# Re-ordering the work on four engines where a first graph network hands over to a second

## The chip, the cores and the metric

The kernel runs on one core of one Trainium2 chip. It is a single launch; the metric is the device time in microseconds (us), and the time given is the median of 3 runs. The engines of the core run their own instruction streams and wait for each other through semaphores: PE (TensorE, matrix products and their weight loads), DVE (VectorE), ACT (ScalarE), POOL (GpSimd) and SP (SyncE, which here only issues DMA transfers).

## The reference

The input is 128 graphs of 64 nodes with 384 features, x, and a 0/1 adjacency matrix per graph. Two networks of two layers each run one after the other, and behind each stands a residual sum with a layer norm:

```python
x = _layernorm(x + _L0_gnn_ref(x, adj, ...), axis=-1)
x = _layernorm(x + _L1_gnn_ref(x, adj, ...), axis=-1)
```

A layer of the first network ("gated") computes two bilinear score matrices of the node features, takes one on and above the diagonal and the other below, multiplies exp(scores) by the adjacency and normalises each row; the result averages a linear map of the features; then a layer norm with its own gain and shift, and relu. A layer of the second network ("softmax") takes scores h h^T / sqrt(384), a softmax masked by the adjacency and normalised again, and adds three products: neighbours above the diagonal with one linear map, below it with a second, and the node itself with a third. Again layer norm, gain, shift, relu. All is float32.

## The kernel before

The 8192 rows (nodes) are cut into 8 passes of 2 streams of 512 rows; a stream is 4 tiles (t) of 128 rows, two graphs in each. A unit is one layer on one stream, so a pass has 4 units: layer 0 of stream 0 and of stream 1, then layer 1 of both. All 8 passes of the first network run, then all 8 of the second. The first network's result goes to the memory tensor x1 and from there into the second.

To keep float32 accuracy, each operand of a product is split into a high half (ACT copies it with rounding) and a low half (the rest, by a subtraction on DVE or POOL), and PE sums three products. So each operand goes through the chain PE, DVE, ACT, POOL before PE may use it, and the program is written so that PE computes the value products of one unit while the others prepare the next. The order on each engine is written out by hand; it changes only where the code is changed. The engines meet at semaphores, and an instruction that waits holds everything behind it on its engine.

Names that matter. In the first network `next_turn(k)` on PE transposes block k (of 3) of the second network's first input (x_in to turn); `next_turn_out(k)` on ACT makes its high half in ht, `next_turn_lo(k)` on DVE its low half. `next_scores` waits for all three.

In the second network a unit has 12 value jobs of 9 matmuls on PE (`values(j)`, L1143): tile t = j div 3, side j mod 3 (upper, lower, own). They go through a ring of 4 work banks. `biased_value(j)` (L1437, DVE) reads a bank, adds the bias and frees it for job j + 4. For the first two sides `values_hi(t)` (L1238, ACT) and `values_lo(t)` (L1329, POOL) make the halves. On PE, jobs 0 to 8 are followed by `turn_block` 0 and 1 of the next unit, job 9, `turn_block` 2, jobs 10 and 11, the next unit's scores, and 4 `contexts` tiles (L1155). `turn_block` 2 (L1104) uses the bank of block 0, and waits for `turn_lo(0)` on DVE (L1416), which waits for `turn_out(0)` on ACT (L1201 in layer 0, L1204 in layer 1). The contexts wait for `values_lo` of their tile. `fold_parts` (L1120, L1123) is PE's first work in a unit. `masks` (L1323, POOL) prepares the adjacency masks for a stream, `diagonal` (L1340) the node's own weight.

Three things of the first network are left over when the second begins. The last stream's context (`gated.variances`, `deviations`, `gain_and_shift`), its residual sum (`add_residual`, L793) and the statistics of the sum (`final_stats`, L798) run on DVE between the first biased values of the second. `residual_and_stats(tiles)` issues for some tiles all the sums, then all the statistics. `final_var` (L802 to L807) collects them, POOL takes the root (`gated_final_roots(1)`, L633), DVE makes the offset (`final_offset`, L811), ACT normalises the rows (`gated_normalise(1)`, L507) and SP stores them.

The second network's layer 1 weights (3 matrices, 0: left, 1: right, 2: own) are loaded and split at this place too. `weight_hi(n)` (L1193, ACT, one instruction) and `weight_lo(n)` (L1313, POOL, three). Weight 2 is loaded into the buffer of weight 0, so SP waits for `weight_lo(0)`:

```python
            sp.wait_ge(folded, 1)
            load_weight(0)
            load_weight(1)
            store_last(0)
            sp.wait_ge(split, 1)
            load_weight(2)
            store_last(1)
            sp.wait_ge(split, SIDES)
```

They are used from unit 2 of the first pass on. Before, `weight_hi(0)`, `(1)` and `(2)` and their low halves all stand in unit 1 of the first pass, beside the first unit's end.

## Time and profile before

| | |
|---|---|
| median of 3 runs | 1760.14 us (1759.49 to 1760.24) |
| the profiled execution | 1760.6 us |
| its span, first to last instruction | 1758.8 us |
| PE matmul busy | 1695.9 us, 96% |
| DVE, ACT, POOL busy | 1255.1, 882.7, 825.3 us (71%, 50%, 47%) |
| mean granted TensorE clock | 0.99 of 2.4 GHz |
| second network's first matmuls | 845.90 us |

The profile is one execution. Its page gives each engine's busy share over the span; the two networks follow each other, so the share is a mean over both, and the place where they meet, from some 840 to 920 us, is about 5% of it. There PE's busy time is 17.65, 13.83, 20.00 and 12.87 us in the four 20 us stretches from 840 to 920. The granted clock is what the chip gave TensorE, as a share of 2.4 GHz: 1.00 or 0.50, and a value between the two where a window holds some of each. In a timeline "[2.35 <-DVE b_ht L711]" means that the engine was idle for 2.35 us before this instruction, ended by the named one.

### The profile page before, as it was taken

Reading aid. Unit: us, or ns where it says so; the run is one execution under the profiler, and the core shown is the slowest. Engines: PE = TensorE matmul, PEld = TensorE weight load, DVE = VectorE, ACT = ScalarE, POOL = GpSimd, SP = SyncE. Lnnn points to the kernel's source line nnn. Section 1 sums busy time; section 2 is a strip of 40 time slices with the busy share of each in tenths; the row PEclk is TensorE's granted clock in tenths of the full one; section 3 lists DMA queues with packets and bytes.
Section 4 is the critical chain, followed back from the end, with each engine's and each line's share of the span. In section 5 each row is a group of like instructions: output and inputs, shape, how many; then the busy total and the mean of one; then the engine's idle time right before and its main releaser. Section 6 shows DMA issues by size and latency. Waiting matters only on the chain.

```text
span 1758.8 us, 30529 instructions
## 1 busy us (share of the span) xinstructions
PE 1695.9 (96%) x9856; PEld 1601.9 (91%) x9856; DVE 1255.1 (71%) x2735; ACT 882.7 (50%) x1785; POOL 825.3 (47%) x860
## 2 busy tenths in 40 slices
PE   7999999999999999999889999999999999999994
PEld 6989989898998988998789999999999999999994
DVE  4587685958768586786846867768677686776766
ACT  4545455464545546455445464454554545544542
POOL 5143242424324243334546646666465664656635
PEclk9999999999999999999899999999999999999997
DMA  7014030020202102030111020201202011020200
GB/s 224 1 31 153 6 104 15 24 89 28 91 6 64 55 24 89 6 114 17 49 50 58 21 92 21 92 0 34 80 21 92 0 54 59 21 92 0 75 1 36
DMA packets 76358, 91.98 MB, mean 52 GB/s; under 512 B 29600, under 2 KB 67488, under 8 KB 76320
## 3 DMA queue, kind: packets, MB, share of 16 engines
q1 hardware_dynamic: 76320, 91.51, 15.7%
q8 instruction: 20, 0.33, 0.1%
q14 instruction: 18, 0.15, 0.0%
HBM read 53.75 MB, written 25.17 MB: 45 GB/s over the span
## 4 chain that ended last, share of the span: by engine, by line
PE 38%; issue 36%; POOL 16%; DVE 4%; ACT 3%; SPq 1%; DMA 1%; POOLq 0%; DVEq 0%; ACTq 0%
PE b_work L1143 24%; PE b_work L1155 5%; POOL g_qv_lo L620 3%; POOL b_ht L600 3%; POOL s_v_lo L1329 3%; PE b_work L355 2%; PE b_turn L1104 2%; PE b_score_ps L105 2%; POOL b_z L1353 1%; PE b_work L379 1%; PE b_score_ps L369 1%; POOL g_keep_l L615 1%; POOL b_z L1355 1%; POOL g_sigma L629 1%; POOL g_a_nat L616 1%
## 5 line engine op out<-in xcount | busy, mean ns | idle before, releaser
L1143 PE MATMUL b_work<-b_w_hi,b_ht 128*128 128x384 f32 x2304 | 615.7, 340 | 0.0
L1143 PEld LDWEIGHTS b_work<-b_w_hi,b_ht 128*128 128x128 f32 x2304 | 420.9, 189 | 0.0
L1143 PE MATMUL b_work<-b_w_lo,b_ht 128*128 128x384 f32 x1152 | 387.4, 336 | 0.0
L355 PE MATMUL b_work<-b_ht,b_w_hi 128*128 128x512 f32 x1152 | 357.7, 392 | 9.8 <-DVE b_w_lo L695 9.8
L1329 POOL TENSOR_TENSOR s_v_lo<-s_v_full,s_v_hi 128x384 fp32r<-128x384 f32 x256 | 247.4, 983 | 198.2 <-ACT s_v_hi L1238 197.4
L620 POOL TENSOR_TENSOR g_qv_lo<-g_v_full,g_qv_hi 128x384 fp32r<-128x384 f32 x128 | 133.2, 1060 | 360.5 <-ACT g_qv_hi L493 360.5
L355 PEld LDWEIGHTS b_work<-b_ht,b_w_hi 128*128 128x128 f32 x1152 | 216.2, 189 | 51.2 <-issue 9.7
L355 PE MATMUL b_work<-b_ht,b_w_lo 128*128 128x512 f32 x576 | 225.9, 392 | 0.0
L1143 PEld LDWEIGHTS b_work<-b_w_lo,b_ht 128*128 128x128 f32 x1152 | 218.1, 189 | 0.0
L718 DVE TENSOR_TENSOR g_qv_lo<-b_work,g_qv_hi 128x512 fp32r<-128x512 f32 x192 | 128.7, 687 | 111.9 <-ACT g_qv_hi L481 110.0
L379 PE MATMUL b_work<-b_w_hi,b_ht 128*128 128x384 f32 x768 | 206.5, 336 | 0.0
L1437 DVE TENSOR_TENSOR s_v_full<-b_work,b_bias 128x384 f32<-128x384 f32 x256 | 140.3, 553 | 81.6 <-PE b_work L1143 81.6
L481 ACT ACTIVATE g_qv_hi<-b_work 128x512 fp32r<-128x512 f32 x192 | 110.6, 591 | 132.2 <-PE b_work L355 132.1
L1238 ACT ACTIVATE s_v_hi<-s_v_full 128x384 fp32r<-128x384 f32 x256 | 129.4, 529 | 86.1 <-DVE s_v_full L1437 86.1
L369 PE MATMUL b_score_ps<-g_qv_hi,b_ht 128*128 128x256 f32 x768 | 146.9, 285 | 4.8 <-DVE g_qv_lo L718 4.8
L379 PEld LDWEIGHTS b_work<-b_w_hi,b_ht 128*128 128x128 f32 x768 | 139.9, 188 | 1.3
L355 PEld LDWEIGHTS b_work<-b_ht,b_w_lo 128*128 128x128 f32 x576 | 108.7, 189 | 23.0
L379 PE MATMUL b_work<-b_w_lo,b_ht 128*128 128x384 f32 x384 | 128.8, 335 | 0.0
L369 PEld LDWEIGHTS b_score_ps<-g_qv_hi,b_ht 128*128 128x128 f32 x768 | 120.6, 188 | 8.5 <-DVE g_qv_lo L718 7.4
L1437 DVE TENSOR_TENSOR s_v_own<-b_work,b_bias 128x384 f32<-128x384 f32 x128 | 71.1, 555 | 65.3 <-PE b_work L1143 64.9
L369 PE MATMUL b_score_ps<-g_qv_lo,b_ht 128*128 128x256 f32 x384 | 107.3, 279 | 0.0
L1244 ACT ACTIVATE b_z<-b_z,s_foffset,s_frstd 128x384 f32<-128x384 f32 x62 | 39.0, 699 | 134.8 <-DVE s_foffset L1533 134.8
(138 smaller groups left out, 3225.0 us busy)
## 6 DMA issues: line engine op xcount, KB each, us to landing
b_x_in<-in_x_t SPq DMA_DIRECT2D x16, 768.0 KB, 7.0
g_x_res<-in_x SPq DMA_DIRECT2D x16, 768.0 KB, 7.7
x<-b_z SPq DMA_DIRECT2D x16, 768.0 KB, 3.9
b_x_in<-x SPq DMA_DIRECT2D x16, 768.0 KB, 5.1
s_x_res<-b_x_in SPq DMA_DIRECT2D x16, 768.0 KB, 5.4
out<-b_z SPq DMA_DIRECT2D x15, 768.0 KB, 3.6
b_a_tr<-in_adj_t SPq DMA_DIRECT2D x64, 64.0 KB, 3.4
g_a_nat<-in_adj SPq DMA_DIRECT2D x32, 64.0 KB, 2.5
```

The costliest lines, as they stand in the source:

```text
L355: mm = pe.matmul(bank[:], w, h, start=(n == 0), stop=(n == len(pairs) - 1))
L369: mm = pe.matmul(score_ps[:, t, :, :], h, q, start=(n == 0), stop=(n == len(pairs) - 1))
L379: mm = pe.matmul(bank[:, 0:H], h, w, start=(n == 0), stop=(n == len(pairs) - 1))
L481: nc.scalar.activation(q_hi[:, m, :, d, :], work[use % RING][:], ACT.Copy).then_inc(q_hi_ready, 1)
L600: nc.gpsimd.tensor_tensor(ht_lo[s][:, k, :], xt_in[s][:, k, :], ht_hi[s][:, k, :].bitcast(F32), ALU.subtract).then_inc(x_split, 1)
L620: nc.gpsimd.tensor_tensor(v_lo[:, t, 0:H], v_full[:, t, :], v_hi[:, t, 0:H].bitcast(F32), ALU.subtract).then_inc(v_lo_ready, 1)
L718: op = nc.vector.tensor_tensor(q_lo[:, m, :, d, :], bank, q_hi[:, m, :, d, :].bitcast(F32), ALU.subtract)
L1143: mm = pe.matmul(bank[:, 0:H], h, w, start=(n == 0), stop=(n == len(pairs) - 1))
L1155: mm = pe.matmul(bank[:, 0:HC], p, v, start=(n == 0), stop=(n == len(pairs) - 1))
L1238: nc.scalar.activation(v_hi[:, t, n, 0:H], v_full[:, (2 * t + n) % VF, :], ACT.Copy)\
L1329: nc.gpsimd.tensor_tensor(v_lo[:, t, n, 0:H], v_full[:, (2 * t + n) % VF, :], v_hi[:, t, n, 0:H].bitcast(F32), ALU.subtract).then_inc(v_lo ...
L1437: nc.vector.tensor_tensor(dst, work[(unit * WN + j) % RING][:, 0:H], bias[:, side, layer, :], ALU.add).then_inc(work_free, 1)
```

## The change

It computes the same values with the same instructions. What moves:

- PE: `next_turn(2)` is issued behind the value job of tile 2, ahead of tile 3's, in place of behind it. ACT's `next_turn_out(2)` goes ahead of the last `value_hi`, and DVE's `next_turn_lo(2)` ahead of `probabilities_lo` and the last biased value.
- DVE: the last residual sums and statistics, issued for tiles (0, 1) behind biased value 5 and (2, 3) behind value 7, are now issued tile by tile: tile 0 behind value 6, tile 1 behind the turned block's third low half, tile 2 behind the row sum `own_probability`, tile 3 with `final_var` in the next unit, behind its first biased value. `final_offset` goes behind that unit's `deviations`. DVE's first pass is written out ahead of its loop for this.
- ACT: `weight_hi(0)` goes to unit 0, behind the high halves of tile 1; `weight_hi(1)` to the end of unit 0, in the place of `gated_normalise(1)`; `gated_normalise(1)` into unit 1 behind `probabilities_hi`, where the two weights had been; `weight_hi(2)` behind the turned blocks' copies and the last high halves.
- POOL: `weight_lo(0)` behind `diagonal` of unit 0, the two low halves of tile 2 and then the masks of stream 1 behind it; `weight_lo(1)` at the end of unit 0, in the place of `gated_final_roots(1)`, which goes behind the first low halves of unit 1.
- SP: the same.

```diff
--- before.py
+++ after.py
@@ -416,10 +416,11 @@
                     for t in range(1, NT):
 
                         value(i, unit, t, uses=1 if more or t < NT - 1 else 2)
+                        if not more and t == 2:
+                            next_turn(2)
                     if more:
                         query(i, unit + 1, 0).then_inc(work_full, 1)
                     else:
-                        next_turn(2)
                         next_scores()
                     contexts(i, unit)
                     if more:
@@ -527,12 +528,12 @@
                 value_hi(i, unit, 1)
                 probabilities_hi(i, unit)
                 value_hi(i, unit, 2)
+                if not more:
+                    next_turn_out(2)
                 value_hi(i, unit, 3)
                 if more:
                     query_hi(i, unit + 1, 0)
                     contexts_out(i, unit)
-                else:
-                    next_turn_out(2)
 
             def one_pass(i, last):
 
@@ -849,10 +850,9 @@
                 biased_value(i, unit, 2)
                 if not more:
                     next_turn_lo(1)
+                    next_turn_lo(2)
                 probabilities_lo(i, unit)
                 biased_value(i, unit, 3, uses=1 if more else 2)
-                if not more:
-                    next_turn_lo(2)
                 if s is not None:
                     for t in range(NT - 1):
                         final_stats(i, s, t)
@@ -1256,19 +1256,18 @@
                 exponentials(i, unit)
                 values_hi(i, unit, 0)
 
-            def second_half(i, unit, more, split_weights):
+            def second_half(i, unit, more, tail):
                 values_hi(i, unit, 1)
                 probabilities_hi(i, unit)
-                if split_weights:
-                    weight_hi(0)
-                    weight_hi(1)
+                if tail:
+                    gated_normalise(1)
                 values_hi(i, unit, 2)
-                if split_weights:
-                    weight_hi(2)
                 if more:
                     for k in range(KO):
                         turn_out(i, unit + 1, k)
                 values_hi(i, unit, 3)
+                if tail:
+                    weight_hi(2)
                 if more:
                     copy_part(i, unit + 1)
 
@@ -1293,11 +1292,13 @@
             gated_normalise(0)
             for t in range(3):
                 values_hi(0, 0, t)
+                if t == 1:
+                    weight_hi(0)
             for k in range(KO):
                 turn_out(0, 1, k)
             values_hi(0, 0, 3)
             copy_part(0, 1)
-            gated_normalise(1)
+            weight_hi(1)
             one_pass(0, False, first=True)
             with act.Fori(1, PASSES - 1) as i:
                 one_pass(i, False)
@@ -1362,14 +1363,13 @@
                     roots(i, unit)
                     if more:
                         values_lo(i, unit + 1, 0)
+                    if first and unit == 0:
+                        gated_final_roots(1)
                     if layer == 1:
                         for t in range(NT // 2 if more else LAST_GT):
                             gain_and_shift(i, s, t)
                     if more:
                         values_lo(i, unit + 1, 1)
-                        if first and unit == 0:
-                            weight_lo(0)
-                            weight_lo(1)
                         diagonal(i, unit + 1)
                     if layer == 1 and more:
                         for t in range(NT // 2, NT):
@@ -1397,10 +1397,11 @@
             values_lo(0, 0, 0)
             values_lo(0, 0, 1)
             diagonal(0, 0)
+            weight_lo(0)
+            values_lo(0, 0, 2)
             masks(0, 1, first=True)
-            values_lo(0, 0, 2)
             values_lo(0, 0, 3)
-            gated_final_roots(1)
+            weight_lo(1)
             one_pass(0, False, first=True)
             with pool.Fori(1, PASSES - 1) as i:
                 one_pass(i, False)
@@ -1569,7 +1570,7 @@
                 if s is not None:
                     final_offset(i, s)
 
-            def one_pass(i, last):
+            def one_pass(i, last, first=False):
 
                 for unit in range(UNITS):
                     layer, s = divmod(unit, STREAMS)
@@ -1579,7 +1580,12 @@
                             maximum(i, unit + 1)
                         for j in range(SIDES):
                             biased_value(i, unit + 1, j)
+                            if first and unit == 0 and j == 0:
+                                gated.residual_and_stats((3,))
+                                gated.final_var()
                         deviations(i, unit)
+                        if first and unit == 0:
+                            gated.final_offset()
                         up_to_contexts(i, unit + 1, last, s if layer == 1 else None)
                     else:
 
@@ -1607,22 +1613,22 @@
             biased_value(0, 0, 4)
             gated.gain_and_shift(3)
             biased_value(0, 0, 5)
-            gated.residual_and_stats((0, 1))
             biased_value(0, 0, 6)
+            gated.residual_and_stats((0,))
             biased_value(0, 0, 7)
-            gated.residual_and_stats((2, 3))
             biased_value(0, 0, 8)
             turn_lo(0, 1, 0)
             turn_lo(0, 1, 1)
-            gated.final_var()
             biased_value(0, 0, 9)
             turn_lo(0, 1, 2)
+            gated.residual_and_stats((1,))
             biased_value(0, 0, 10)
             own_probability(0, 0)
+            gated.residual_and_stats((2,))
             biased_value(0, 0, 11)
             contexts_out(0, 0)
-            gated.final_offset()
-            with dve.Fori(0, PASSES - 1) as i:
+            one_pass(0, False, first=True)
+            with dve.Fori(1, PASSES - 1) as i:
                 one_pass(i, False)
             one_pass(PASSES - 1, True)
```

PE at the end of the first network's last unit, the piece of the difference (L379 is a value job, L401 `next_turn`, L105 the second network's scores, L390 contexts):

```order
 L379 MATMUL b_work<-b_w_hi,b_ht 128x384
 L401 MATMUL b_turn<-b_const,b_x_in 128x128 x4
+L379 MATMUL b_work<-b_w_hi,b_ht 128x384
+L379 MATMUL b_work<-b_w_lo,b_ht 128x384
+L379 MATMUL b_work<-b_w_hi,b_ht 128x384 x2
+L379 MATMUL b_work<-b_w_lo,b_ht 128x384
+L379 MATMUL b_work<-b_w_hi,b_ht 128x384 x2
+L379 MATMUL b_work<-b_w_lo,b_ht 128x384
+L379 MATMUL b_work<-b_w_hi,b_ht 128x384
 L105 MATMUL b_score_ps<-b_ht 128x256 x12
```

The four transposes of block 2 stand one value job of nine matmuls earlier; before, this last job stood ahead of them, and now it stands between them and the scores.

DVE in unit 0 of the second network, from biased value 5 on; before:

```order
L1437 TENSOR_TENSOR s_v_own<-b_work,b_bias 128x384
L793 SCALAR_TENSOR_TENSOR b_z<-b_z,g_x_res 128x384 x2
L798 BN_STATS g_fstats<-b_z 128x6 x2
L1437 TENSOR_TENSOR s_v_full<-b_work,b_bias 128x384 x2
L793 SCALAR_TENSOR_TENSOR b_z<-b_z,g_x_res 128x384 x2
L798 BN_STATS g_fstats<-b_z 128x6 x2
L1437 TENSOR_TENSOR s_v_own<-b_work,b_bias 128x384
L1416 TENSOR_TENSOR b_ht<-b_turn,b_ht 128x512 x2
L802 MEMSET g_fvar 128x4
L804 BN_AGGR g_fmv<-g_fstats 128x2 x4
L807 TENSOR_TENSOR g_fvar<-g_fvar,g_fmv 128x4
```

and after (its lines are one higher):

```order
L1438 TENSOR_TENSOR s_v_own<-b_work,b_bias 128x384
L1438 TENSOR_TENSOR s_v_full<-b_work,b_bias 128x384
L794 SCALAR_TENSOR_TENSOR b_z<-b_z,g_x_res 128x384
L799 BN_STATS g_fstats<-b_z 128x6
L1438 TENSOR_TENSOR s_v_full<-b_work,b_bias 128x384
L1438 TENSOR_TENSOR s_v_own<-b_work,b_bias 128x384
L1417 TENSOR_TENSOR b_ht<-b_turn,b_ht 128x512 x2
L1438 TENSOR_TENSOR s_v_full<-b_work,b_bias 128x384
L1417 TENSOR_TENSOR b_ht<-b_turn,b_ht 128x512
L794 SCALAR_TENSOR_TENSOR b_z<-b_z,g_x_res 128x384
L799 BN_STATS g_fstats<-b_z 128x6
L1438 TENSOR_TENSOR s_v_full<-b_work,b_bias 128x384
```

Between biased value 5 and the turned blocks' first low halves (L1416, now L1417) stand four residual sums (L793) and four statistics (L798) before, and one of each now; two more of each follow it, and the fourth stands in the next unit.

ACT from the copy of the score parts at the end of unit 0 (L1213, behind the last high halves L1238) to the turned block of unit 2 (L1204); before:

```order
L1213 ACTIVATE b_part<-b_score_ps 64x4x64 x2
L507 ACTIVATE b_z<-b_z,g_foffset,g_frstd 128x384 x4
L1220 ACTIVATE b_turn<-b_score_ps 128x512
L1226 ACTIVATE s_expo,s_exp_sum<-b_score_ps 128x128 x4
L1238 ACTIVATE s_v_hi<-s_v_full 128x384 x2
L1252 ACTIVATE b_z<-b_z,s_offset,s_rstd 128x384 x4
L1238 ACTIVATE s_v_hi<-s_v_full 128x384 x2
L1233 ACTIVATE s_prob_hi<-b_turn 128x512 x2
L1193 ACTIVATE b_w_hi<-s_x_res 128x1152 x2
L1238 ACTIVATE s_v_hi<-s_v_full 128x384 x2
L1193 ACTIVATE b_w_hi<-s_x_res 128x1152
L1204 ACTIVATE b_ht<-b_turn,b_shift_f,b_gain_f 128x512
```

and after:

```order
L1238 ACTIVATE s_v_hi<-s_v_full 128x384 x2
L1213 ACTIVATE b_part<-b_score_ps 64x4x64 x2
L1193 ACTIVATE b_w_hi<-s_x_res 128x1152
L1220 ACTIVATE b_turn<-b_score_ps 128x512
L1226 ACTIVATE s_expo,s_exp_sum<-b_score_ps 128x128 x4
L1238 ACTIVATE s_v_hi<-s_v_full 128x384 x2
L1252 ACTIVATE b_z<-b_z,s_offset,s_rstd 128x384 x4
L1238 ACTIVATE s_v_hi<-s_v_full 128x384 x2
L1233 ACTIVATE s_prob_hi<-b_turn 128x512 x2
L508 ACTIVATE b_z<-b_z,g_foffset,g_frstd 128x384 x4
L1238 ACTIVATE s_v_hi<-s_v_full 128x384 x2
L1204 ACTIVATE b_ht<-b_turn,b_shift_f,b_gain_f 128x512
```

The weight splits (L1193) before all stand in unit 1, the third directly ahead of the turned block's copies (L1204). Now the first stands in unit 0, ahead of these rows, the second behind the copy of the score parts (L1213), and the third is behind the six rows of L1204; the first network's last normalisation (L507, now L508) stands where two of them were.

## Rows read from the trace of the kernel before

**Rows 1.** The waits, 835 to 925 us: engine line waited for: total us, times, longest.
```profile
PE b_turn L1104 <- DVE b_ht L1416: 13.3, 2, 7.1
...
ACT b_w_hi L1193 <- DMA s_x_res<-in_L_gnn_Ws: 5.6, 1, 5.6
```

**Rows 2.** Windows of 2 us; after the engines' busy times: granted clock, DMA share, GB/s.
```profile
846.00:848.00 2.00, 2.00 (x11) 2.00 (x12) 1.23 (x3) 0.00 (x0) 2.00 (x2) 0.57 0.00 0
...
872.00:874.00 2.00, 0.00 (x0) 0.00 (x0) 2.00 (x5) 0.00 (x0) 1.26 (x2) 0.90 0.00 0
...
912.00:914.00 2.00, 2.00 (x8) 2.00 (x8) 1.14 (x3) 1.80 (x3) 0.00 (x0) 0.50 0.00 0
```

**Rows 3.** The timeline of PE: start us, us, line, operation, count, [idle before].
```profile
842.95 0.60 PE L401 MATMUL b_turn<-b_const,b_x_in 128*128 128x128 f32 x4
845.90 2.63 PE L105 MATMUL b_score_ps<-b_ht 128*128 128x256 f32 x12 [2.35 <-DVE b_ht L711]
...
851.07 0.40 PE L1120 MATMUL b_score_ps<-b_part,b_eye_r 128*128 128x256 f32 x2
...
874.58 1.11 PE L1104 MATMUL b_turn<-b_const,b_x_in 128*128 128x128 f32 x4 [6.17 <-DVE b_ht L1416]
875.34 0.67 PE L1143 MATMUL b_work<-b_w_hi,b_ht 128*128 128x384 f32 x1
...
880.89 1.59 PE L105 MATMUL b_score_ps<-b_ht 128*128 128x256 f32 x12
...
911.04 1.12 PE L1104 MATMUL b_turn<-b_const,b_z 128*128 128x128 f32 x4 [7.13 <-DVE b_ht L1416]
911.81 0.67 PE L1143 MATMUL b_work<-b_w_hi,b_ht 128*128 128x384 f32 x1
...
916.31 1.59 PE L105 MATMUL b_score_ps<-b_ht 128*128 128x256 f32 x12
```

**Rows 4.** The chain of waits: start us, us, what, count; all at full clock.
```profile
881.05 1.43 PE b_score_ps L105 x12
882.48 4.25 PE b_work L1155 x24
...
887.36 9.45 PE b_work L1143 x54
```

**Rows 5.** The timeline of DVE, 835 to 880 us.
```profile
835.73 1.96 DVE L793 SCALAR_TENSOR_TENSOR b_z<-b_z,g_x_res 128x384 f32<-128x384 f32 x4
...
861.20 0.54 DVE L1437 TENSOR_TENSOR s_v_full<-b_work,b_bias 128x384 f32<-128x384 f32 x1
...
865.75 2.75 DVE L793 SCALAR_TENSOR_TENSOR b_z<-b_z,g_x_res 128x384 f32<-128x384 f32 x2
...
872.46 1.01 DVE L798 BATCH_NORM_STATS2 g_fstats<-b_z 128x6 f32<-128x384 f32 x2
...
873.84 1.27 DVE L1416 TENSOR_TENSOR b_ht<-b_turn,b_ht 128x512 fp32r<-128x512 f32 x2
```

**Rows 6.** The timeline of POOL, 840 to 925 us.
```profile
845.53 3.75 POOL L1323 TENSOR_TENSOR s_keep<-b_a_tr,b_const 128x512 f32<-128x512 f32 x3
852.12 1.01 POOL L633 TENSOR_TENSOR g_frstd<-g_fvar,g_powers 128x4 f32<-128x4 f32 x1 [2.84 <-DVE g_fvar L807]
...
917.03 2.97 POOL L1313 TENSOR_TENSOR b_w_lo<-s_x_res,b_w_hi 128x384 fp32r<-128x384 f32 x3
```

**Rows 7.** The timeline of ACT, 880 to 925 us.
```profile
888.32 2.50 ACT L507 ACTIVATE b_z<-b_z,g_foffset,g_frstd 128x384 f32<-128x384 f32 x4 [5.04 <-DVE g_foffset L811]
...
899.12 2.21 ACT L1193 ACTIVATE b_w_hi<-s_x_res 128x1152 fp32r<-128x1152 f32 x2
901.23 0.93 ACT L1238 ACTIVATE s_v_hi<-s_v_full 128x384 fp32r<-128x384 f32 x2
...
908.86 0.76 ACT L1204 ACTIVATE b_ht<-b_turn,b_shift_f,b_gain_f 128x512 fp32r<-128x512 f32 x1
```

**Rows 8.** The timeline of PE at the end of a unit, near 1002 us.
```profile
1002.78 0.44 PE L1155 MATMUL b_work<-s_v_hi,s_prob_hi 128*128 128x386 f32 x1 [0.78 <-POOL s_v_lo L1329]
```

## The prediction

> **What bounds the kernel now.** The busy table and the 40 slices say the matrix engine (PE, TensorE) is busy 96% of the span, and that one slice in the middle is lower than its neighbours. Away from that slice only a change that shortens PE's own work could matter, and this change adds and removes none of it. So I read the waits of the stretch 835 to 925 us, where the first network hands over to the second. There PE waits for VectorE (DVE): 13.3 us in two pieces ahead of turned blocks alone [rows 1]. PE's timeline dates these two and a third: stall A, 2.35 us, ahead of the second network's first scores at 845.90; stall B, 6.17 us, ahead of the third turned block of the next unit at 874.58; stall C, 7.13 us, ahead of the same block one unit later at 911.04 [rows 3]. The windows add a second cost: behind A and C the granted clock is 0.57 and 0.50 while PE is fully busy, so 1.2 GHz in place of 2.4 GHz, and in B it begins to fall at 872 to 874, 0.90 [rows 2].
>
> **Size of the three stalls with their clock.** At full clock 12 score matmuls take 1.43 us, 24 context matmuls 4.25, and 54 value matmuls 9.45, so 1.57 for a value job of 9 [rows 4]. Behind A the 12 scores and 12 context matmuls fill 845.90 to 851.07, 5.17 us, against 1.43 + 2.12 = 3.55: 1.62 lost [rows 3, 4]. Behind B four transposes take 0.76 (0.40 at full clock) and 18 value matmuls 5.55 (3.15), so 2.76 lost. Behind C 0.77 and 4.50, so 1.72 lost [rows 3]. In all A 3.97, B 8.93, C 8.85: 21.75 us. That is the most the change can give, since PE is the bound before and after, and a microsecond saved here is not waited for again.
>
> **A: next_turn(2) one value job earlier on PE, with its copy and its low half earlier on ACT and DVE.** Before, the low half waited for transposes issued at 842.95 and, on ACT, stood behind the last value's high half. Now they start a value job earlier, at 842.95 - 1.57 = 841.4 [rows 3]. ACT is free for the copy once the high half of value 2 is done, which waits for that value and two operations of 0.5: near 842.7. The copy, 0.55, and DVE's subtraction, 0.6, make it 843.85. PE, which does the same work in another order, is free at 843.55 (842.95 + 0.60). Left over is 0.3 us, and with so short a stall I let the clock stay up: a stall of 0.78 us at a unit's end has no window of low clock behind it [rows 8]. PE gains 2.0 + 1.6 = 3.6 us. DVE's chain gains less. Value 3's low half on POOL, which had ended at 845.53, ends some 0.8 later; the three masks behind it take 3.75, and then the root of 1.01 that had started at 852.12 starts at 850.1 [rows 6]. So DVE enters the second network 1.95 us earlier, PE 3.6 earlier, and part of A comes back: the fourth biased value ended at 861.75 [rows 5] and will end near 859.8, where PE's value job 7 could start at 859.05. 0.75 us left.
>
> **B: residual and statistics.** Four residual adds and four statistics are spread. Before, DVE did 2 adds in 2.75 at 865.75, 2 statistics, 2 biased values, and again 2 adds, 2 statistics and a biased value (these three 1.38 from start to start, 0.46 each), before the turned block's subtraction at 873.84 [rows 5]. Ahead of that subtraction now stands one add with its statistics: three adds at 1.37 and three statistics at 0.46 are gone from it: 5.5 us. The fifth biased value ends near 865.75 - 1.95 = 863.8; then biased value 6 (0.46), add (1.37), statistics (0.46), biased value 7 (0.46) reach 866.55. ACT's high half of that value, 0.45, and its copy of the turned block, 0.5, come next on ACT, as in the old order, then DVE's 0.6: 868.2. PE, whose job 9 starts at 863.8, is idle from 865.4. Left over: 2.8 us of 6.17. The add was not seen in this place beside POOL's weight split. Its bounds are 0.49 (four in 1.96 with POOL idle) and 1.37 (half of 2.75 with POOL on its masks) [rows 5]; POOL will be on the weight split there, so I take 1.37. At the other end, if DVE's chain gains nothing from A, the first leftover grows by 1.95 to 2.7.
>
> The Trainium skill, SBUF — State Buffer, section "Who interferes with whom", says that a VectorE instruction with two SBUF inputs and a GpSimd instruction that reads SBUF block each other for a whole instruction. By it the spread speaks against itself: the tiles 1 and 2 that now stand beside POOL's masks delay POOL too. The trace agrees with the DVE half of it: 1.37 an add against 0.49. By the rule this makes the rival on POOL below more likely; the sum here would move by 0.1.
>
> The moved adds of tiles 1 and 2 stand behind biased values 9 and 10 and cost 3.7 us in all before biased value 11. From 868.2 the chain is two subtractions, two biased values, a subtraction, these 3.7 and the row sum of 0.7: done near 875.2. The last context tile, which needs that bank, comes on PE at 868.2 + 0.4 + 2 x 1.57 + 1.43 + 3 x 1.06 = 876.4. Covered, by 1.2. Tile 3's add, 0.5 and 0.46, and the variance, 0.55, stand in the next unit behind its first biased value, where DVE had waited about 1 us for each value job.
>
> **C: weight splits.** Before, ACT split weights 0 and 1 at 899.12 in 2.21 [rows 7], POOL took 2.97 for its half of a weight [rows 6], and only then could SP load weight 2 into weight 0's buffer. ACT stood 5.6 us at that load [rows 1] with the turned block's copies queued behind it, DVE behind ACT, PE behind DVE. Now ACT splits weight 0 in the unit before, where it waits for biased value 6, POOL's half of it ends near 867.5, and weight 2, even at the 5.6 us that ACT stood for it, is in by 873, more than 20 us ahead of need; its split comes behind the copies. In its old place stands the normalisation of the first network's last rows (2.50, as at 888.32 [rows 7]). That is 0.3 longer than the two splits it replaces. With the high halves of 0.93 behind it, as at 901.23, and then the copy pair (2 x 0.67) and the subtraction [rows 5, 7], the turned block is ready about 0.8 after PE's job 9 ends. Left over: 0.8. Weight 2's low half, 2.97 on POOL, is due 8 us after its split: covered. The new wait on DVE, for the root of the last tile, holds biased values 3 on, and POOL has two low halves ahead of the root: about 1.5 us, against 4 or more that PE's four banks cover.
>
> **Sum.** 21.75 - 0.3 - 0.75 - 2.8 - 0.8 = 17.1 us. Then the clock. A stall of 2.35 us was followed by the low clock and 1.6 lost, one of 0.78 was not [rows 2, 3, 8]; the new 2.8 is nearest to the first, so I charge 1.6. The Trainium skill, TensorE: Matmul & The Clock Gate, section "What's actually happening", says that the default state is throttled and activity releases it; without any drop the gain would be 17.1. 15.5 us from the profiled 1760.6 is 1745.1; the median of the runs is 0.46 below the profiled run, so 1744.6.
>
> **The rivals.**
> 1. The clock stays up in the 2.8 us stall: 1743.0. For it: the drop behind B came only some 5 us into it [rows 2], so a stall's length alone does not decide.
> 2. POOL takes the place of DVE. Its queue in unit 0 is now diagonal, weight split (2.97), two low halves, masks (3.75), two low halves (0.99 each, the shape of a third of the weight split [rows 6]): from 864.5 on, 10.6 us, to 875.1, and with the stretch that DVE's adds give it to 876, and PE wants the last at 876.4. With the moved adds in its way it is late by 1 or 2 us, with biased values 10 and 11 late behind it and a second clock drop: a gain of 10 to 13, so 1749.
> 3. Only C goes. The copies of the turned block still wait for biased value 7, and if the adds are as slow as seen and DVE's chain gains nothing, A and B give 1 or 2 together: a gain of about 9, 1751.6. Against it: three adds simply are no longer there.
> 4. The change doesn't shift the time: PE catches up elsewhere anyway. Against it: PE is 96% busy and has no other stall over 1 us until its end. 1760.
> 5. Slower: DVE stands at the new wait for the last root, with biased values 3 on queued behind it. POOL's root waits there for two low halves, these for ACT's high halves, these for DVE's biased value 1. The calculated wait is 1.5 us; it costs from about 5.4 on and makes the kernel slower only from 5.4 + 15.5 = 21 us on; with 25, 1764.5. Nothing in the rows is that long.
>
> **How the numbers follow.** The forecast has 0.45, rival 1 0.30, rival 2 0.14, rival 3 0.06, rival 4 0.02, rival 5 0.03. The range goes from 1741.5 (rival 1 with an add of 0.49 in B and nothing left in C) to 1750 (rival 2); rival 3 and what is beyond it are left out, a good 1 in 10, and something for both edges. Within 0.2% (3.5 us, what a measurement of this kernel tells from no change) is rival 4; faster 0.95, same 0.02, slower 0.03.
>
> **What would show it.** In the profile after, PE's three stalls should read about 0.3, 2.8 and 0.8, with one below 1 us near the second network's value job 7; ACT's wait for the DMA of weight 2 is gone; the clock is below 1 at most once there. Fold matmuls behind unit 1 should come about 17 us earlier than 922 if the clock stays up, and 15.5 if it falls once. A wait of PE's context matmuls for POOL's low halves would speak for rival 2; a third-block stall above 5 us for rival 3; a DVE wait for the first network's last root above 5 us for rival 5.

## The result, and the profile after

| | us, median (lowest to highest) | profiled run | its span |
|---|---|---|---|
| before | 1760.19 (1759.49 to 1760.44, 4 runs) | 1760.6 | 1758.8 |
| changed | 1749.28 (1749.11 to 1750.89, 4 runs) | 1750.89 | 1749.1 |

The ratio is 0.9941, 95% interval 0.9923 to 0.9958: 10.9 us faster, where 15.5 were forecast. The forecast was 1744.6, 4.7 us lower than measured, with a range to 1750.0. The profiled run is the slowest of the four, 1.6 us above their median.

The waits of the changed kernel from 835 to 925 us, those that answer to [rows 1], and its first new one:

```profile
PE b_turn L1104 <- DVE b_ht L1417: 2.8, 3, 2.0
...
DVE g_foffset L812 <- POOL g_frstd L634: 2.2, 2, 1.3
...
PE b_work L1143 <- DVE s_v_full L1438: 0.5, 1, 0.5
...
PE b_score_ps L105 <- DVE b_ht L712: 0.4, 1, 0.4
```

The 13.3 us ahead of turned blocks are 2.8, and ACT's wait for a weight's DMA, 5.6 us before, has no row any more. PE's timeline of the changed kernel dates what is left, as [rows 3] did before:

```profile
844.68 1.70 PE L105 MATMUL b_score_ps<-b_ht 128*128 128x256 f32 x12 [0.41 <-DVE b_ht L712]
...
868.61 0.76 PE L1104 MATMUL b_turn<-b_const,b_x_in 128*128 128x128 f32 x4 [2.04 <-DVE b_ht L1417]
...
873.80 1.59 PE L105 MATMUL b_score_ps<-b_ht 128*128 128x256 f32 x12
...
897.42 0.66 PE L1104 MATMUL b_turn<-b_const,b_z 128*128 128x128 f32 x4 [0.58 <-DVE b_ht L1417]
```

Stall A is 0.41 us (2.35 before), B 2.04 (6.17), C 0.58 (7.13). The windows of the changed kernel (columns as in [rows 2]) show that the clock stays up behind A and C and falls behind B alone:

```profile
846.00:848.00 2.00, 2.00 (x15) 2.00 (x14) 1.30 (x4) 1.76 (x5) 1.63 (x2) 1.00 0.00 0
...
868.00:870.00 2.00, 1.39 (x7) 1.39 (x8) 1.61 (x3) 0.92 (x3) 2.00 (x3) 0.76 0.27 25
870.00:872.00 2.00, 2.00 (x8) 2.00 (x7) 1.94 (x3) 0.41 (x1) 2.00 (x3) 0.50 0.76 270
872.00:874.00 2.00, 2.00 (x12) 2.00 (x12) 2.00 (x4) 0.53 (x1) 2.00 (x2) 0.89 0.01 4
...
898.00:900.00 2.00, 2.00 (x13) 2.00 (x12) 1.58 (x3) 1.86 (x3) 0.00 (x0) 1.00 0.00 0
```

From the block of B at 868.61 to the scores at 873.80 PE's work takes 5.19 us. The same work takes 3.63 us in a later kernel whose clock stayed up there (871.92 to 875.55, shown below). So the low clock behind B cost about 1.6 us.

VectorE's timeline of the changed kernel around B and at the new wait, against [rows 5]:

```profile
865.03 0.71 DVE L794 SCALAR_TENSOR_TENSOR b_z<-b_z,g_x_res 128x384 f32<-128x384 f32 x1
...
867.86 1.29 DVE L1417 TENSOR_TENSOR b_ht<-b_turn,b_ht 128x512 fp32r<-128x512 f32 x2 [0.61 <-ACT b_ht L1201]
...
870.64 1.32 DVE L794 SCALAR_TENSOR_TENSOR b_z<-b_z,g_x_res 128x384 f32<-128x384 f32 x1
...
887.14 0.16 DVE L812 SCALAR_TENSOR_TENSOR g_foffset<-g_fmv,g_frstd 128x4 f32<-128x4 f32 x1 [0.98 <-POOL g_frstd L634]
```

**What the hand-over gave.** The same 12 score matmuls stand well behind the hand-over and five passes on. PE's timeline, kernel before, then changed kernel:

```profile
1105.85 1.59 PE L105 MATMUL b_score_ps<-b_ht 128*128 128x256 f32 x12
...
1649.93 1.59 PE L105 MATMUL b_score_ps<-b_ht 128*128 128x256 f32 x12
```

```profile
1090.50 1.59 PE L105 MATMUL b_score_ps<-b_ht 128*128 128x256 f32 x12
...
1639.94 1.59 PE L105 MATMUL b_score_ps<-b_ht 128*128 128x256 f32 x12
```

The first one comes 15.35 us earlier. The changed kernel's profile was late by 0.71 before anything of the change ran: VectorE's four adds, at 835.73 before [rows 5], stand at 836.44. So the hand-over gave 16.1 us in this profile; 15.5 were forecast. Five passes on only 9.99 us are left: five passes take 549.44 us in place of 544.08, 5.36 more. In those passes nothing was meant to change.

VectorE's waits from 900 to 1740 us have a row that the kernel before has not:

```profile
DVE s_total L1481 <- issue: 11.2, 5, 2.4
```

"Issue" is standing for nothing that the profile shows. VectorE's timeline of the changed kernel has one of the five:

```profile
1101.45 0.32 DVE L1534 SCALAR_TENSOR_TENSOR s_foffset<-s_fmv,s_frstd 128x4 f32<-128x4 f32 x1
1103.98 0.17 DVE L1481 SCALAR_TENSOR_TENSOR s_total<-s_exp_sum,b_z 128x4 f32<-128x4 f32 x1 [2.21 <-issue]
```

It is the edge of VectorE's loop over the passes. In the kernel before these two follow at once, and PE's waits of 900 to 1740 us have no row for value matmuls at all. In the changed kernel PE, one bank ring further, waits each time (here at 1105.27):

```profile
PE b_work L1143 <- DVE s_v_full L1438: 4.0, 5, 0.9
```

The DMA view of 900 to 1740 us, before and then changed, says what moves at such an edge (packets, MB, share):

```profile
q14 instruction: 8, 0.07, 0.0%
```

```profile
q14 instruction: 35, 0.29, 0.1%
```

27 more instruction packets of about 8 KB, some 5 for each of the five edges. From 1110 to 1690 us, where nearly everything is passes of the loop, this queue has 1 packet before and 22 in the changed kernel. At the edge shown above one of them falls within the standing (window of 1102 to 1103 us); the others of a pass come later in it, and nothing waits for them. Five packets are 40 KB a pass. The view doesn't name the engine whose instructions they are: that they are VectorE's is taken from their coming and going with its standing.

### The profile page after: what moved, and what is told of

Read it like the earlier page. It is cut to its first block, busy times and chain, and to the rows that moved or that the text cites. A ratio compares the mean times of both kernels' runs of the same rounds, so it can differ in the third digit from the quotient of the medians.

```text
span 1749.1 us, 30427 instructions
## 1 busy us (share of the span) xinstructions
PE 1694.3 (97%) x9856; PEld 1597.7 (91%) x9856; DVE 1253.8 (72%) x2735; ACT 883.8 (51%) x1785; POOL 824.5 (47%) x860
## 4 chain that ended last, share of the span: by engine, by line
PE 40%; issue 35%; POOL 13%; DVE 8%; ACT 3%; SPq 1%; DMA 0%; POOLq 0%; DVEq 0%; ACTq 0%
PE b_work L1143 25%; PE b_work L1155 5%; POOL g_qv_lo L621 3%; POOL b_ht L601 3%; PE b_work L355 2%; PE b_turn L1104 2%; PE b_score_ps L105 2%; DVE b_z L1515 1%; DVE b_z L1472 1%; POOL s_v_lo L1330 1%; PE b_score_ps L369 1%; PE b_work L379 1%; POOL g_keep_l L616 1%; POOL g_sigma L630 1%; POOL g_a_nat L617 1%
## 5 line engine op out<-in xcount | busy, mean ns | idle before, releaser
L379 PE MATMUL b_work<-b_w_hi,b_ht 128*128 128x384 f32 x768 | 206.6, 336 | 0.0
L1238 ACT ACTIVATE s_v_hi<-s_v_full 128x384 fp32r<-128x384 f32 x256 | 129.4, 528 | 84.5 <-DVE s_v_full L1438 84.5
L379 PEld LDWEIGHTS b_work<-b_w_hi,b_ht 128*128 128x128 f32 x768 | 139.8, 188 | 1.2
L379 PE MATMUL b_work<-b_w_lo,b_ht 128*128 128x384 f32 x384 | 128.6, 335 | 0.0
```

The costliest lines, as they stand in the source:

```text
L379: mm = pe.matmul(bank[:, 0:H], h, w, start=(n == 0), stop=(n == len(pairs) - 1))
L1238: nc.scalar.activation(v_hi[:, t, n, 0:H], v_full[:, (2 * t + n) % VF, :], ACT.Copy)\
```

## Experiments: the loop's edge

The change writes VectorE's first pass out ahead of its loop, which then starts at pass 1. In the built program the loop is 312 instructions; it begins at instruction 473 of VectorE's program before and at 683 after, 210 further on.

**The written-out pass alone**, on the kernel before:

```diff
-            with dve.Fori(0, PASSES - 1) as i:
+            one_pass(0, False)
+            with dve.Fori(1, PASSES - 1) as i:
```

> The kernel before with one edit: VectorE's first pass of the second network is written out ahead of its loop, all work in the old order. Theory F (the written-out pass puts the loop at a place in the program where its instructions are fetched again in each pass): no gain at the hand-over, each of the 5 loop edges costs about 1.07 us as in the changed kernel, so 1760.2 + 5.4 = 1765.6 us, with DVE standing 2.2 us behind the last final_offset of each pass and five 8 KB instruction fetches per pass. Rival G (the 5 us of the later passes come from the moved sums, splits or transfers): 1760.2, same as before, no such stall.

Measured 1765.67 us (8 runs), ratio 1.003 (1.0019 to 1.004). So the same work in the same order, with one pass written out, is 5.3 us slower. The row of the waits is back:

```profile
DVE s_total L1480 <- issue: 11.0, 5, 2.2
```

**The changed kernel with no loop at all** on VectorE (every pass written out):

```diff
-            with dve.Fori(1, PASSES - 1) as i:
+            for i in range(1, PASSES - 1):
```

> The changed kernel with VectorE's loop over the second network's passes written out in full. Theory F: a stream without a branch has no edge to stall at, the five stalls go and the time is 1749.3 - 5.4 = 1743.9 us, with more instruction fetches but none that is waited for. Rival G: 1749.3. A third theory (fetches cost something wherever they fall, not at the branch): 1749 or more.

1744.91 us, ratio 0.991 (0.9895 to 0.9925). No standing, and the 4.4 us between this and the changed kernel are the price of the edges in the median of runs. It is within 0.3 us of the time that the prediction gave the changed kernel (1744.6). From 1110 to 1690 us this kernel has 9 instruction packets of 8 KB: written-out code is fetched too, but VectorE's longest wait for "issue" there is 0.2 us.

**The changed order without a written-out pass**, as a difference from the changed kernel: tile 3's sum, statistics and variance stand ahead of VectorE's reading of the contexts, the offset behind it, the last root on POOL behind the second weight half, and the loop starts at pass 0:

```diff
+            gated.residual_and_stats((3,))
+            gated.final_var()
             contexts_out(0, 0)
-            one_pass(0, False, first=True)
-            with dve.Fori(1, PASSES - 1) as i:
+            gated.final_offset()
+            with dve.Fori(0, PASSES - 1) as i:
```

> The changed kernel with VectorE's loop as before, from pass 0: the last tile's sum, statistics and variance stand ahead of unit 0's contexts_out, the offset behind it, POOL's last root behind weight_lo(1). All other moves stay. Theory F: the loop is back to within some ten instructions of its old place, no stalls at its edges, the hand-over gains about 15.8 as in the changed kernel: 1744 us. Rival G: 1749. If the place of tile 3's work matters itself, the hand-over shows it: DVE's contexts_out comes 1.5 us later, PE's banks cover it.

1744.62 us, ratio 0.9909 (0.9894 to 0.9925); no standing, with the loop at instruction 475. One new stall of PE pays for the four sums in one place: 0.67 us ahead of value matmuls at 879.64, released by VectorE's reading of the contexts. The same kernel a second time:

> The version without a written-out pass once more, for the comparison with the other two on the same chip: 1744.6 us, ratio to the kernel before 0.991. Whether the clock falls behind the stall of 2.04 us is open: it did not in its first profile, and did in that of the version with the loop written out, where the stall was 2.06 us.

1744.51 us, ratio 0.991 (0.9894 to 0.9927).

**Is it the written-out pass, or the place that it moves the loop to?** Two kernels move the loop by small VectorE writes at the very start, where VectorE stood until 6.14 us:

```diff
+            for k in range(80):
+                nc.vector.memset(pad[:, k:k + 1], 0.0)
```

> The kernel before with 80 small VectorE writes of zeros to a spare row at its very start, where VectorE stood until 6.1 us anyway; nothing else differs, and no pass is written out ahead of the loop. VectorE's loop of the second network has 312 instructions of 64 bytes; it begins at instruction 473 of VectorE's program in the kernel before and at 553 here. 
> The changed kernel with 64 small VectorE writes to a spare row at its very start, under VectorE's first wait; VectorE's pass 0 of the second network stays written out ahead of the loop. The loop begins at instruction 747 instead of 683, half a line of 8 KB further (0.84 of a line instead of 0.34). Theory F (place of the loop): the standing at the loop's ends goes, and with it 5 x 1.07 us: 1744 us, as with the loop written out entirely (1744.9). Rival P (the written-out pass itself): nothing changes, 1749.3 us and 2.2 us of standing at each end.

The 80 writes on the kernel before gave 1770.41 us (1768.93 to 1771.58), ratio 1.0063 (1.0049 to 1.0077), with the standing there though nothing was written out. The 64 writes on the changed kernel gave 1747.49 us (1747.08 to 1750.65), ratio 0.9936 (0.9922 to 0.9949), with no standing though a pass was written out. The waits of the first, and the instruction packets of 900 to 1740 us of the first and of the second:

```profile
DVE s_total L1483 <- issue: 13.4, 6, 2.3
```

```profile
q14 instruction: 39, 0.32, 0.1%
```

```profile
q14 instruction: 11, 0.09, 0.0%
```

Two numbers of the expectations missed. There were six edges of standing, not seven: the loop runs 7 times and has 6 ways back. And both times are higher than expected, by 4.8 and by 3.5 us, since the writes were not free: in both kernels PE's first scores of the second network come 3.3 to 3.5 us later, before the loop in question begins. So the second network is better taken by itself: from those scores to the end of the span, and, cleaner still, over five passes of the loop, between the same 12 score matmuls as above. PE's timelines of the kernel with 80 writes and of the one with 64:

```profile
1108.79 1.59 PE L105 MATMUL b_score_ps<-b_ht 128*128 128x256 f32 x12
...
1658.23 1.59 PE L105 MATMUL b_score_ps<-b_ht 128*128 128x256 f32 x12
```

```profile
1092.35 1.59 PE L105 MATMUL b_score_ps<-b_ht 128*128 128x256 f32 x12
...
1636.42 1.59 PE L105 MATMUL b_score_ps<-b_ht 128*128 128x256 f32 x12
```

| kernel | loop begins at | first scores | span | from one to the other | five passes | edges with standing |
|---|---|---|---|---|---|---|
| before | 473 | 845.90 | 1758.8 | 912.9 | 544.1 | 0 |
| before, pass written out | 681 | 846.10 | 1763.9 | 917.8 | 549.3 | 5 |
| before, 80 writes | 553 | 849.40 | 1767.1 | 917.7 | 549.4 | 6 |
| changed | 683 | 844.68 | 1749.1 | 904.4 | 549.4 | 5 |
| changed, 64 writes | 747 | 848.02 | 1745.3 | 897.3 | 544.1 | 0 |
| changed, no loop | none | 844.69 | 1742.9 | 898.2 | 543.6 | 0 |

Five passes take 549.3 or 549.4 us with the standing, 544.1 with a loop that does not stand, and 543.6 with no loop. So an edge with standing costs 1.04 to 1.07 us, and a loop without standing some 0.4 us in five passes against none. The column before it (4.9 and 4.8 us lost where the standing appeared, 7.1 and 6.2 gained where it went) also holds how the clock fell out: with 80 writes it stayed up behind stall A (12 scores in 1.70 us, 2.63 before), with 64 behind B, 1.6 us each. Place decides, not the written-out pass. The loop stood at 681, 683 and 553, and did not at 473, 475 (the version without a written-out pass) and 747. Counted in lines of 128 instructions (8 KB, the size of the packets, if an instruction is 64 bytes), the loop of 2.44 lines begins at 0.32, 0.34 and 0.32 of a line where it stood, at 0.70, 0.71 and 0.84 where it did not; that fits lines whose borders lie so that the first three touch one line more. Counted from the program's first instruction they would touch one fewer (0.32 + 2.44 ends in the third line, 0.70 + 2.44 in the fourth), so the borders would have to lie 0.34 to 0.70 of a line off, and no run shows where they lie. Counted in blocks of 256 it stood at 0.66, 0.67 and 0.16 and did not at 0.85, 0.86 and 0.92; a loop of 1.22 blocks would touch a third block over an arc of 0.22 only, and 0.66 and 0.16 can't both lie in it, so blocks would fit only if touching fewer were the worse case. So the six places show that place decides, but not by which rule; how many lines are held isn't shown either.

The Trainium skill, Runtime: NRT & Kernel Launch, section "Instruction fetch mechanics", says that a taken branch whose target is not in the two pages just held forces a fetch before execution goes on. The trace agrees with that: packets of the instruction queue and 2.2 us of standing at a way back, and none without one. It gives the pages as 16 KiB, 256 instructions each. The packets of this queue are of 8 KB (those of the other instruction queue, q8, are of 16 KB: 8 in 0.13 MB), and blocks of 256 fit the six places only if touching fewer were the worse case. For VectorE's packets the measurement decides.

## Experiments: the three stalls

**Third place alone**: only the weights' splits, and the last normalisation that changes places with them, are moved on ScalarE and GpSimd.

```diff
-                if split_weights:
-                    weight_hi(0)
-                    weight_hi(1)
+                if tail:
+                    gated_normalise(1)
...
+                if t == 1:
+                    weight_hi(0)
...
             diagonal(0, 0)
-            masks(0, 1, first=True)
+            weight_lo(0)
             values_lo(0, 0, 2)
+            masks(0, 1, first=True)
             values_lo(0, 0, 3)
+            weight_lo(1)
```

> The kernel before with the weight splits and the last normalisation moved on ACT and POOL as in the changed kernel, and nothing on PE or DVE (POOL's last root behind weight_lo(1)). Term C alone: stall C of 7.13 us and its 1.72 of low clock go but for about 0.6: gain 8.2, so 1752.0 us. If stalls A and B hid part of C or the other way round, the gain is under 6.

1750.91 us (5 runs), ratio 0.9942 (0.9929 to 0.9956): C is 0.60, A unchanged at 2.37, B 5.65. One place of three gives 9.5 us, 1.3 more than expected, of which 0.5 is B's. It is as fast as the changed kernel to within 1.7 us, since its loop does not stand.

**First place alone**, here PE's part; ScalarE's copy and VectorE's low half move with it as in the change:

```diff
                         value(i, unit, t, uses=1 if more or t < NT - 1 else 2)
+                        if not more and t == 2:
+                            next_turn(2)
...
-                        next_turn(2)
                         next_scores()
```

> The kernel before with the first place alone mended: TensorE turns the last block of the second network's first input ahead of the last value product of the last unit, ScalarE copies it and VectorE subtracts it ahead of their last work for that product. The stall of 2.35 us ahead of the first scores goes to about 0.4. Theory (VectorE's chain of residual sums and offsets decides the next stall): VectorE's sums come only as much earlier as its waits in that stretch were TensorE's, so the second stall takes over most of it, and the low clock behind the first stall (0.57 in one slice of 2 us, about 1.6 us lost with what lies beside it) goes too: gain 1.9 us, 1758.4. If the second stall didn't take it over, 4.0 us of gain: 1756.3. If it took all of it: 1760.3.

1759.0 us (11 runs), ratio 0.9994 (0.9985 to 1.0003): no difference that can be told. The medians differ by 0.8 us; the interval reaches from 2.6 us faster to 0.5 slower, so it holds the 1.9 expected and excludes the 4.0 of a stall that nothing takes over. The stall went as expected, and the next one grew. PE's timeline of this kernel:

```profile
844.13 1.69 PE L105 MATMUL b_score_ps<-b_ht 128*128 128x256 f32 x12 [0.41 <-DVE b_ht L712]
...
872.84 1.12 PE L1104 MATMUL b_turn<-b_const,b_x_in 128*128 128x128 f32 x4 [6.77 <-DVE b_ht L1416]
...
907.92 1.11 PE L1104 MATMUL b_turn<-b_const,b_z 128*128 128x128 f32 x4 [7.10 <-DVE b_ht L1416]
```

A gave 1.9 us of stall, B took 0.6 of it, value job 7 0.53, and the clock fell behind B and behind C as before.

**Second place alone**:

```diff
             biased_value(0, 0, 6)
-            gated.residual_and_stats((0, 1))
+            gated.residual_and_stats((0,))
             biased_value(0, 0, 7)
...
```

and so on, as in the version without a written-out pass.

> The kernel before with the second place alone mended: VectorE's sums and statistics of the first network's last residual one tile at a time between the biased values, tile 3 and the variance behind the last of them; no pass written out, the first and third place as before. The stall of 6.2 us (8.9 with its low clock) goes to 1.6 to 2.0 us, and if the clock then falls all the same 1.5 us stay lost by it. Theory (the three stalls add up as they were costed): gain 7 us, 1753.2; with the clock drop staying 1754.5. Rival: the third stall (7.2 us, waited for through POOL's weight half) takes over what is gained here, since POOL is not earlier: gain near 0, 1760.

1753.19 us (5 runs), ratio 0.9964 (0.9951 to 0.9978). B is 1.86 us, and C stays at 7.02: it does not take over what B gave. In this profile the clock stayed up behind A too, a stall of 2.36 us, and behind B. 9.5 + 0.8 + 6.7 = 17.0 us for the three apart; together, in the version without a written-out pass, 15.8 and 16.2 in its two comparisons: they add up to about 1 us, and the intervals leave more open than that.

**The rest of B.** On the changed kernel without VectorE's loop, the turned blocks go ahead of all sums:

```diff
             biased_value(0, 0, 6)
-            gated.residual_and_stats((0,))
             biased_value(0, 0, 7)
-            biased_value(0, 0, 8)
             turn_lo(0, 1, 0)
             turn_lo(0, 1, 1)
+            biased_value(0, 0, 8)
             biased_value(0, 0, 9)
             turn_lo(0, 1, 2)
-            gated.residual_and_stats((1,))
+            gated.residual_and_stats((0,))
...
```

with ScalarE's turned blocks ahead of its third value half, GpSimd's fourth low half ahead of the masks and its second weight half in the next unit, and two sums in the next unit.

> The changed kernel with VectorE's loop written out (1744.9 us as measured) and the rest of the second stall taken away: VectorE subtracts turned blocks 0 and 1 ahead of the first residual sum, sums of tiles 2 and 3 and the variance come between the biased values of the next unit, ScalarE copies the turned blocks ahead of the next value half, GpSimd makes the last weight half only in the next unit. Theory (the 2.04 us left of the second stall stand because of VectorE's one residual sum and statistics ahead of the turned blocks, 1.3 us, and of ScalarE's value half, 0.6 us): the stall is under 0.3 us, the clock does not fall behind it, and 1.8 to 3.1 us are gained: 1741.8 us. Rival (VectorE's work to the first contexts is the bound of this stretch, so PE waits there what it no longer waits here): 1744.5 us with a new stall of 1.5 to 2 us for VectorE's reading of the contexts or the next biased value.

1740.72 us (1740.33 to 1741.13), ratio 0.9888 (0.9871 to 0.9904): the best of all. B is gone, and with it its low clock. PE's timeline:

```profile
866.42 0.60 PE L1104 MATMUL b_turn<-b_const,b_x_in 128*128 128x128 f32 x4
...
869.99 1.59 PE L105 MATMUL b_score_ps<-b_ht 128*128 128x256 f32 x12
```

In the kernel without a loop these stand at 868.62 and 873.81. So the block comes 2.2 us earlier, and the work from it to the scores takes 3.57 us in place of 5.19, 1.6 us of clock: 3.8 in all. The expectation had stopped at 3.1.

The same, but with all sums ahead of the contexts, as it must be without a written-out pass, and GpSimd's order as in the change:

> The same order up to the turned blocks, but no pass written out: all four sums, statistics and the variance stand ahead of VectorE's reading of the contexts, as in the version without a written-out pass (1744.6 us), and GpSimd's order stays that of the change. Theory (here VectorE's work to the first contexts is the bound): of the 2.04 us of the second stall 0.9 us are VectorE's own waiting and are gained, the other 1.1 us come back where PE waits for VectorE to free the bank of the contexts, 0.67 us before, 1.8 us now: 1743.7 us. Rival (the work fits): 1742.6 us.

1743.72 us, ratio 0.9907 (0.9891 to 0.9924): the expected time for another reason. PE does not wait for VectorE's bank there; it waits for GpSimd. PE's and POOL's timelines of this kernel:

```profile
876.86 0.44 PE L1155 MATMUL b_work<-s_v_hi,s_prob_hi 128*128 128x386 f32 x1 [2.22 <-POOL s_v_lo L1331]
```

```profile
870.21 4.43 POOL L1325 TENSOR_TENSOR s_keep<-b_a_tr,b_const 128x512 f32<-128x512 f32 x3
874.61 2.13 POOL L1331 TENSOR_TENSOR s_v_lo<-s_v_full,s_v_hi 128x384 fp32r<-128x384 f32 x2
```

The 2 us taken from B come back as 2.22 us behind the masks; what is gained over the version without a written-out pass, 0.8 us, is about the 0.67 us stall that this one has no more. That GpSimd's order alone makes this wait was not tried apart from the sums, which differ too.

**The clock behind B, twice.** The kernel without a loop has a B of 2.06 us, the one without a written-out pass of 2.04. The window of 870 to 872 us of the one and of the other:

```profile
870.00:872.00 2.00, 2.00 (x8) 2.00 (x7) 1.97 (x3) 0.32 (x1) 2.00 (x3) 0.50 0.71 262
```

```profile
870.00:872.00 2.00, 2.00 (x14) 2.00 (x13) 1.79 (x2) 0.59 (x2) 2.00 (x3) 1.00 0.75 261
```

The same stall, once at 1.2 GHz behind it and once at 2.4. Both profiles of the second order kept 1.00 throughout. But it is not the order that decides: the changed kernel with 64 writes has the changed kernel's own order here, a B of 2.06 us, and kept 1.00 as well. Its PE timeline and the window between:

```profile
871.92 0.66 PE L1107 MATMUL b_turn<-b_const,b_x_in 128*128 128x128 f32 x4 [2.06 <-DVE b_ht L1420]
...
875.55 1.59 PE L105 MATMUL b_score_ps<-b_ht 128*128 128x256 f32 x12
```

```profile
874.00:876.00 2.00, 2.00 (x14) 2.00 (x14) 1.97 (x3) 0.00 (x0) 2.00 (x2) 1.00 0.58 217
```

Stall A goes the same way: 2.35 us in the kernel before with a low clock behind it, 2.33 with 80 writes and 2.36 with the sums alone without one. What decides between them stays open.

## Why the prediction was right and wrong

- **What bounds the kernel**: right for the hand-over. Three stalls and their clock, 21.75 us, were where the gain lay; 16.1 of it came in the profile, 15.5 were forecast. The time itself lies inside the range only by luck: the range's upper edge, and the 1749 close to which the time came (1749.28), belong to rival 2, whose mechanism did not occur.
- **A**: 0.41 left, 0.3 forecast, clock up as assumed. Much of its gain comes back, as the text said of VectorE's chain: taken alone the first place is worth 0.8 us by the medians, 2.6 at most.
- **Value job 7**: 0.50 left, 0.75 forecast.
- **B**: 2.04 left, 2.8 forecast. The mis-sized term is the add next to the weight split: 0.71 us, not 1.37. Its 0.66 did not all come through: with the profile's lateness of 0.71 taken off, the block stands at 867.90, 0.3 ahead of the forecast 868.2, and the rest is that PE ran dry at 865.9 and not at 865.4. The moved adds beside the masks took 1.32 and 1.25, near the 1.37 of before. Rival 1 was not the profiled run, since the clock fell and cost 1.6 us, as charged. That the charge came out is luck too: the kernel with 64 writes, with the same order and stall, kept its clock.
- **C**: 0.58 left, 0.8 forecast. VectorE's new wait for the last root is 0.98 us at 887.14, 1.5 forecast, and PE waits for nothing behind it.
- **Rival 2** (POOL takes VectorE's place) did not occur here: PE's waits have no row for POOL's low halves in the hand-over. It was close: with PE 2 us earlier it is a 2.22 us stall.
- **The step that failed** is in the first paragraph: "Away from that slice only a change that shortens PE's own work could matter, and this change adds and removes none of it." What was saved at the hand-over was indeed not waited for again there, but the passes behind it did not stay as they were. The sum priced only the instructions that the change moves. It gave no price to VectorE's first pass written out ahead of its loop, which does not alter one instruction's order but shifts the loop by 210 instructions. That cost 5 edges at 1.07 us, 5.36 us of the profiled run; 5.3 by the written-out pass alone (1765.67 against 1760.39), 4.4 by taking the loop away. None of the five rivals had it either.
- **The profiled run's sum closes**: 1750.89 - 1745.1 = 5.8 us too low. 5.36 is the loop; 0.71 was lost before the change's first instruction; 0.6 more than forecast came at the hand-over; the stretch behind 1649.93 (1639.94 after) is 0.3 longer. 5.36 + 0.71 - 0.6 + 0.3 = 5.8. The median missed by less, 4.7, because the profiled run stood 1.6 above it, where the forecast had taken 0.46.

## What to carry to other kernels

A diff can cost time in a place that it does not touch: where code is written out ahead of a hardware loop, look, on the engine concerned, at the waits for "issue" at the loop's edge and at the count of instruction packets, before and after, and price the ways back. When stalls follow each other down a chain of engines, price each by taking it alone: the first was worth some 1 us, 2.6 at most, though it looked like 4; the others kept most of theirs. What such a place has left (here 3.8 us with its clock) goes by putting what PE waits for ahead of what nobody waits for on all of its engines; leave one out and the wait moves there.

## What the runs showed of the hardware

- A loop of 312 VectorE instructions stands at every way back or at none, by where it begins: 2.2 us of standing and about five 8 KB instruction packets a pass against none. Of each 2.2 PE loses 1.04 to 1.07 us; its banks cover the rest.
- 80 and 64 VectorE writes of 128x1 at the start, beneath an idle stretch, were followed by a first network 3.5 and 3.3 us longer. VectorE's loop of that network had moved too. Why it is longer stays open.
- The same stall of 2.04 to 2.06 us is followed by 1.2 GHz in some kernels and not in others, even with the same order of work.
